# Three fp32r products in more places, context by columns, two load queues and another order in a fused attention and mixture-of-experts layer

## The chip, the cores and the metric
One core of one Trainium2 chip runs the kernel as one program. The metric is the device time of an execution in microseconds; lower is better. The engines are PE (TensorE, matmuls; its weight loads are listed as PEld), DVE (VectorE), ACT (ScalarE), POOL (GpSimd) and SP (SyncE, which here issues most DMAs). Each engine runs its own instructions in the order in which they are written, and semaphores tie the engines together.

## The reference
x is (32, 64, 128), that is 2048 tokens of width 128, in 32 sequences of 64. The context has the same shape. All is float32.

```python
# cross attention, 8 heads of width 128, q from layernorm(x), k and v from the context
q, k, v = xn @ Wq[h], ctx @ Wk[h], ctx @ Wv[h]            # per head h
A = softmax(mask(q @ k.T)); o = concat_h(A @ v); proj = o @ Wo
x1 = layernorm(ctx + proj) * gamma[0] + beta[0]
ffn = relu(x1 @ W1 + b1) @ W2 + b2                         # 128 -> 256 -> 128
x2 = x + layernorm(x1 + ffn) * gamma[1] + beta[1]
# mixture of experts on m = layernorm(x2)
scores = sigmoid(m @ router_w.T)                           # 16 experts in 4 groups
pick the best 2 groups, then the best 4 experts; combine = their scores, normalised, x 2.5
routed = sum_e combine[:, e] * ((silu(m @ gate_w[e]) * (m @ up_w[e])) @ down_w[e])
shared = silu(m @ sh_gate_w) * (m @ sh_up_w) @ sh_down_w   # two more "experts" of width 128
out = x2 + routed + shared
```

## The kernel before
**Tiling.** The 2048 tokens are 16 tiles of 128 (n = 0 to 15) and 4 chunks of 512 (c = 0 to 3). Everything stays in SBUF. Each engine's program is written out by hand as one list of calls of small helpers (`key`, `scores`, `attend`, `up`, `down`, ...), and each helper waits on counts of semaphores. So the order of work on an engine is the order of this list, and what an engine finds not ready holds up all behind it.

**Weights folded.** `fold` (PE) multiplies Wq with Wk and Wv with Wo per head. For the first product DVE's `centre` takes the mean off, ACT's `fold_high` rounds the result to fp32r (the high part) and DVE's `fold_low` subtracts to get the low part. `three` is a product in three fp32r passes, high x high, high x low and low x high, in place of one plain float32 matmul, which the profile lists as two instructions:

```python
pe.matmul(dst, w_hi, m_hi, start=start, stop=False)
pe.matmul(dst, w_hi, m_lo, start=False, stop=False)
return pe.matmul(dst, w_lo, m_hi, start=False, stop=stop)
```

**Attention.** Per chunk: POOL's `mask_context` multiplies the context rows by the mask, PE's `turn_ctx` transposes them (4 transposes), ACT's `cT_high` and DVE's `cT_low` split them, and `key(c, h)` makes the keys of head h with `three` (ACT copies each out of its bank, of which there are two). Per tile: `scores` (PE), `mask` and `maximum` (DVE), `subtract_max` (POOL), `exponent` (ACT), `sum_of_exp` (DVE), `normalise_probs` (POOL), `turn_probs` (PE transposes), `spread` (ACT copy), `attend` (PE, on context rows and on a copy with halves swapped), `heads_out` (ACT copies), `project` (PE), `add_ctx` (DVE). SRING = 3 score buffers are in use.

**Between attention and experts**, per chunk: `statistics(1)` (DVE), `inverse_root` (POOL), `normalise` (ACT), `turn_x1` (PE transposes into the post bank; ACT copies with a bias), `ffn_up(c, 0)` and `ffn_up(c, 1)` (PE, each followed by ACT's `hidden`), `ffn_down` (PE), `add_ffn`, `statistics(2)`, `residual`, `statistics(3)` (DVE), `normalise(3)`, `turn_xm` (PE transposes), `take_xm` (ACT copy), `route` (PE, router logits), `take_logits` (DVE), `mT_high` (ACT) and `mT_low` (DVE), the split of the transposed rows. Chunks 0 and 1 are routed together, then 2 and 3: `router_sigmoid` (ACT), `bias_scores`, `group_scores`, `keep_groups`, `keep_experts`, `combine` (DVE, some 45 small operations), `turn_combine` (PE), `take_combine` (DVE), a DMA to DRAM, and DMAs back that spread each expert's row over all partitions.

**Experts.** 18 experts (2 shared, 16 routed) x 4 chunks make N = 72 steps. Steps 0 to 35 do chunks 0 and 1, steps 36 to 71 chunks 2 and 3. The first four steps of a half are the shared experts: (0, c), (1, c), (0, c+1), (1, c+1); so step 2 is the first that needs chunk 1's rows. `up(n)` (PE) makes gate and up, each with `three` (6 passes); `gate` (ACT, silu), `gate_up` (DVE, product), for a routed expert `weigh` (POOL, times the combine weights), and `down(n)` (PE) into the chunk's bank. `up(n)` waits for the split `mT_low` of its chunk, and its second half for `gate_up(n - 2)`; `weigh(n)` waits for `down(n - 4)`. Down is a plain matmul up to step 35 and in the last three steps; in steps 36 to 68 it is `three`, for which ACT's `act_high` and DVE's `act_low` split its input and `dn_high` / `dn_low` the weights:

```python
return SPLIT_FROM <= n < SPLIT_TO     # 36 <= n < 69
```

**Loads.** ACT's queue issues context chunk 0, x by columns, and four quarters of w_in[0]. SP's queue waits for the second quarter and then issues x, context chunk 1, the mask, w_in[1] (two halves), the swapped context and the rest, last the staged expert weights w_gu and w_dn.

Of the kernel before, what the change touches and what calls it, by code (L numbers as in the profile page):

```python
# [57 lines left out]
def build(nc, x, x_cols, ctx_in, mask_tok, mask_pairs, w_attn, w_gu, w_dn, small, w1, w2, vec, out):  # L58
    es = ExitStack()
    with es:  # L60
# [23 lines left out]
        ctx_m = sb("ctx_m", [P, TPC, P])  # L84
# [190 lines left out]
        SPLIT_TO = N - 3  # L275

        def split(n):

            return SPLIT_FROM <= n < SPLIT_TO

        def split_count(n):

            return n - SPLIT_FROM + 1
# [35 lines left out]
        def _(sp):  # L319
# [1637 lines left out]
```

## Time and profile before
| | us |
|---|---|
| median of 3 runs | 296.77 (296.45 to 297.09) |
| the profiled execution, whole | 296.44 |
| its span, first to last instruction | 294.7 |
| PE busy | 285.2 (97%) |
| POOL busy | 183.4 (62%) |
| DVE busy | 178.1 (60%) |
| ACT busy | 161.0 (55%) |

The span is what the profile shows of an execution. The chain of waits follows the last instruction back to what released it, step by step; 88% of the span on it is PE. A timeline row gives the start, the duration, and in brackets how long the engine was idle ahead of it and what ended that. Durations of matmuls overlap (a pass of 0.39 us starts 0.23 us after the one ahead), so what a matmul costs PE is read from start to start. PE's granted clock is 1.00 (2.4 GHz) in every stretch.

### The profile page before, as it was taken

Reading aid. Unit: us, or ns where it says so; the run is one execution under the profiler, and the core shown is the slowest. Engines: PE = TensorE matmul, PEld = TensorE weight load, DVE = VectorE, ACT = ScalarE, POOL = GpSimd, SP = SyncE. Lnnn points to the kernel's source line nnn. Section 1 sums busy time; section 2 is a strip of 40 time slices with the busy share of each in tenths; the row PEclk is TensorE's granted clock in tenths of the full one; section 3 lists DMA queues with packets and bytes.
Section 4 is the critical chain, followed back from the end, with each engine's and each line's share of the span. In section 5 each row is a group of like instructions: output and inputs, shape, how many; then the busy total and the mean of one; then the engine's idle time right before and its main releaser. Section 6 shows DMA issues by size and latency. Waiting matters only on the chain.

```text
span 294.7 us, 4502 instructions
## 1 busy us (share of the span) xinstructions
PE 285.2 (97%) x1427; PEld 207.0 (70%) x1427; DVE 178.1 (60%) x476; ACT 161.0 (55%) x298; POOL 183.4 (62%) x167
## 2 busy tenths in 40 slices
PE   2999999999999999999999999999999999999995
PEld 2765667757776778867766766767668888888882
DVE  0757663837864775876654356397755766656561
ACT  2656667485578476955525352734274455555541
POOL 2136957446757487172758778766706788778871
PEclk9999999999999999999999999999999999999999
DMA  6899400000020000301762432320037236323202
GB/s 212 233 349 271 187 0 3 0 0 2 6 104 0 3 1 0 109 0 54 214 243 71 142 125 90 142 73 4 0 100 262 80 138 214 125 98 137 71 2 71
DMA packets 9575, 29.01 MB, mean 98 GB/s; under 512 B 1232, under 2 KB 2256, under 8 KB 9424
## 3 DMA queue, kind: packets, MB, share of 16 engines
q1 hardware_dynamic: 8688, 27.15, 27.5%
q10 hardware_dynamic: 864, 1.57, 1.6%
q8 instruction: 12, 0.20, 0.3%
q14 instruction: 11, 0.09, 0.1%
HBM read 27.54 MB, written 1.18 MB: 97 GB/s over the span
## 4 chain that ended last, share of the span: by engine, by line
PE 88%; DMA 4%; DVE 3%; ACT 1%; SPq 1%; issue 1%; ACTq 0%; DVEq 0%
PE bank L1449 16%; PE bank L1450 15%; PE bank L1451 15%; PE bank L1528 10%; PE bank L1655 10%; PE bank L1516 6%; PE bank L1488 6%; DMA w_in<-in_w_attn 4%; PE bank L1497 3%; PE bank L1557 3%; PE bank L1550 3%; PE bank L1579 1%; PE bank L1570 1%; PE bank L1543 1%; PE bank L1663 1%
## 5 line engine op out<-in xcount | busy, mean ns | idle before, releaser
L499 POOL TENSOR_TENSOR k_T<-x_T,k_T 128x512 f32<-128x512 f32 x64 | 94.2, 1480 | 41.8 <-DVE x_T L1229 23.1
L764 ACT ACTIVATE x_T<-bank 128x512 f32<-128x512 f32 x72 | 42.7, 598 | 69.5 <-PE bank L1451 68.4
L1229 DVE TENSOR_TENSOR x_T<-bank,x_T 128x512 f32<-128x512 f32 x64 | 43.7, 689 | 50.8 <-ACT x_T L764 27.6
L1449 PE MATMUL bank<-mT_hi,we_hi 128*128 128x512 f32 x144 | 62.7, 435 | 0.1
L1450 PE MATMUL bank<-mT_lo,we_hi 128*128 128x512 f32 x144 | 56.9, 395 | 0.0
L1451 PE MATMUL bank<-mT_hi,we_lo 128*128 128x512 f32 x144 | 56.9, 395 | 0.0
L1655 PE MATMUL bank<-k_T,w_in 128*128 128x512 f32 x78 | 36.6, 594 | 0.0
L1449 PEld LDWEIGHTS bank<-mT_hi,we_hi 128*128 128x128 f32 x144 | 27.1, 188 | 9.7 <-issue 3.8
L1528 PEld LDWEIGHTS bank<-vo,o_T 128*128 128x128 f32 x256 | 30.2, 192 | 4.2 <-issue 3.0
L1450 PEld LDWEIGHTS bank<-mT_lo,we_hi 128*128 128x128 f32 x144 | 27.1, 188 | 8.2 <-issue 2.9
L1528 PE MATMUL bank<-vo,o_T 128*128 128x128 f32 x256 | 31.9, 278 | 0.0
L1451 PEld LDWEIGHTS bank<-mT_hi,we_lo 128*128 128x128 f32 x144 | 27.0, 188 | 6.5
L666 ACT COPY k_T<-bank 128x512 f32<-128x512 f32 x32 | 18.7, 590 | 15.1 <-PE bank L1451 14.0
L421 POOL TENSOR_TENSOR sc_m<-sc_m,nmax 128x512 f32<-128x512 f32 x16 | 17.0, 1065 | 11.2 <-DVE nmax L1085 11.2
L1234 DVE TENSOR_TENSOR act_lo<-k_T,act_hi 128x512 fp32r<-128x512 f32 x33 | 22.5, 682 | 1.6 <-ACT act_hi L773 1.6
L429 POOL TENSOR_TENSOR prob<-sc_m,rsum 128x512 f32<-128x512 f32 x16 | 16.6, 1044 | 10.4 <-DVE rsum L1092 6.4
L695 ACT COPY o_T<-bank 128x512 f32<-128x512 f32 x32 | 17.9, 588 | 8.9 <-PE bank L1516 8.8
L1655 PEld LDWEIGHTS bank<-k_T,w_in 128*128 128x128 f32 x78 | 14.2, 190 | 11.4 <-issue 10.3
L405 POOL TENSOR_TENSOR rstd<-var_eps,neg_half 128x4 f32<-128x4 f32 x12 | 12.3, 1028 | 14.9 <-DVE var_eps L1048 14.9
L773 ACT CAST act_hi<-k_T 128x512 fp32r<-128x512 f32 x33 | 20.3, 614 | 0.3 <-DVE k_T L1229 0.3
L1078 DVE SCALAR_TENSOR_TENSOR sc_m<-bank,rstd_in,mask_add 128x512 f32<-128x512 f32 x16 | 12.0, 748 | 13.1 <-PE bank L1488 9.9
L1516 PE MATMUL bank<-prob_T,ctx_all 64*128 64x256 f32 x64 | 18.2, 402 | 0.0
(127 smaller groups left out, 486.1 us busy)
## 6 DMA issues: line engine op xcount, KB each, us to landing
k_T<-comb_dram SPq DMA_DIRECT2D x32, 512.0 KB, 3.7
w_in<-in_w_gu SPq DMA_DIRECT2D x3, 768.0 KB, 4.6
w_in<-in_w_dn SPq DMA_DIRECT2D x1, 1152.0 KB, 15.7
w_in<-in_w_attn ACTq DMA_DIRECT2D x4, 256.0 KB, 4.7
w_in<-in_w_attn SPq DMA_DIRECT2D x2, 512.0 KB, 7.6
ctx_swap<-in_ctx_in SPq DMA_DIRECT2D x2, 384.0 KB, 13.1
out_x<-ctx_all SPq DMA_DIRECT2D x3, 256.0 KB, 4.6
x_all<-in_x SPq DMA_DIRECT2D x2, 256.0 KB, 5.7
```

Source lines behind the costliest of these rows:

```text
L499: pool.tensor_tensor(act[n % 4], s_u[n % 2], comb[u % RING][:, c % 2 * CW:(c % 2 + 1) * CW], ALU.mult).then_inc(weighed_ready, 1)
L666: a.copy(k_T[c % 2][:, :, h, :], key_bank[i][:].rearrange("p (b s) -> p b s", s=SEQ)).then_inc(key_free[i], 1)
L764: a.activation(silu[n % 2], h_bank[n % 2][:], ACT.Silu).then_inc(silu_ready, 1)
L773: a.copy(act_hi[n % LAG][:], act[n % 4]).then_inc(act_hi_ready, 1)
L1229: v.tensor_tensor(into, u_bank[n % 2][:], silu[n % 2], ALU.mult).then_inc(s_u_ready, 1)
L1234: v.tensor_tensor(act_lo[n % LAG][:], act[n % 4], act_hi[n % LAG][:].bitcast(F32), ALU.subtract).then_inc(act_lo_ready, 1)
L1449: pe.matmul(dst, w_hi, m_hi, start=start, stop=False)
L1450: pe.matmul(dst, w_hi, m_lo, start=False, stop=False)
L1451: return pe.matmul(dst, w_lo, m_hi, start=False, stop=stop)
L1516: last = pe.matmul(o_bank[j][:].rearrange("p (h b s) -> p h b s", b=2, s=SEQ)[:, :, s, :], held[rows, n, :], prob_T[n % 2][rows, :, s, :], ...
L1528: last = pe.matmul(av_bank[:, 0:P], o_T[n % 2][:, h % 2, h // 2, :], vo[:, h, :], start=(h == 0), stop=(h == NH - 1))
L1655: pe.matmul(acc[c][:], dn[:, e, :], act[n % 4], start=start, stop=stop).then_inc(down_full, 1)
```

## The change
It makes five edits. (1) Steps 10 to 23 get the down product in three fp32r passes as well, with `act_high` and `act_low` for them. (2) The 8 `ffn_up` do the same: `w1_high` and `w1_low` split the weights once, and per chunk ACT writes `x1_hi` and a new DVE operation `x1_low` the rest. (3) Context chunks 1 to 3 are loaded by columns, already transposed, with the mask spread over the partitions by DMA; `turn_ctx` is left for chunk 0 alone, and `cT_high`/`cT_low` read SBUF. (4) Context chunk 0 goes first on SP's queue, and ACT's queue begins with the weights. (5) The lists of calls of all engines are in another order. Buffers are shared to make room (`ctx_m` with `xm_T`, `qk_c` with a `cen` buffer).

```diff
-        SPLIT_TO = N - 3
+        SPLIT = [*range(10, 24), *range(SPLIT_FROM, N - 3)]
...
         sp:
+            context(0, 1, ld_c0)
             sp.dma_start(mask_col[:], mask_tok).then_inc(ld_mask_col, 16)
+            def context_columns(c):
+                now = slice(c * CW, (c + 1) * CW)
+                if c > 1:
+                    sp.wait_ge(cT_ready, c - 1)
+                sp.dma_start(mask_r[:], mask_row[now].partition_broadcast(P)).then_inc(ld_cols[c], 16)
+                sp.dma_start(ctx_t[:], ctx_cols[:, now]).then_inc(ld_cols[c], 16)
             rows(0, 1, ld_x0)
-            context(1, 2, ld_c1)
+            context_columns(1)
...          (mask, w_in[1], swapped(0), rows(1), columns(1))
+            context(1, 2, ld_c1)
             context(2, CH, ld_c)
...          (the rest, small_T)
+            context_columns(2)
             sp.wait_ge(fold_done, 6)
...          (w_gu first batch, w_dn)
+                    context_columns(3)
...
         pool:
-            mask_context(0) mask_context(1) inverse_root(0, 0) mask_rows() mask_context(2)
+            mask_context(0) group_order() mask_context(1) mask_rows() inverse_root(0, 0)
...
+            normalise_probs(2) mask_context(2) normalise_probs(3) subtract_max(4)
...
         scalar:
-            a.dma_start(ctx_all[:, 0:TPC, :], ctx_in[:, 0:TPC, :]).then_inc(ld_c0, 16)
-            a.dma_start(x_T[:, 0:CW], x_cols[:, 0:CW]).then_inc(ld_xt[0], 16)
             for q in range(HP):
                 quarter(q)
+            a.dma_start(x_T[:, 0:CW], x_cols[:, 0:CW]).then_inc(ld_xt[0], 16)
...
-                a.activation(x1_T[:], post_bank[:], ACT.Identity, bias=bet[:, 0:1]).then_inc(post_free, 1)
+                a.activation(x1_hi[:], post_bank[:], ACT.Identity, bias=bet[:, 0:1]).then_inc(x1_hi_ready, 1)
+            def w1_high():
+                a.wait_ge(ld_ffn, 32)
+                a.copy(w1_hi[:], w1_in[:]).then_inc(w1_hi_ready, 1)
...
         vector:
+            def w1_low():
+                v.wait_ge(w1_hi_ready, 1)
+                v.tensor_tensor(w1_lo[:], w1_in[:], w1_hi[:].bitcast(F32), ALU.subtract).then_inc(w1_lo_ready, 1)
+            def x1_low(c):
+                v.wait_ge(x1_hi_ready, c + 1)
+                v.scalar_tensor_tensor(x1_lo[:], post_bank[:], bet[:, 0:1], x1_hi[:].bitcast(F32), ALU.add, ALU.subtract
+                                       ).then_inc(post_free, 1)
...
-            centre(0) cT_low(0) fold_low(0) centre(1) fold_low(1) centre(2) fold_low(2) centre(3) fold_low(3)
+            centre(0) fold_low(0) centre(1) cT_low(0) centre(2) fold_low(1) fold_low(2) centre(3) fold_low(3)
...          (hand-over to the experts)
+            statistics(3, 1) add_ctx(14) gate_up(0) add_ctx(15) statistics(1, 3) take_logits(1) gate_up(1)
+            mT_low(1) bias_scores(0) x1_low(2) group_scores(0) gate_up(2) keep_groups(0) keep_experts(0)
+            combine(0) take_combine(0) add_ffn(2) gate_up(3) statistics(2, 2) gate_up(4) x1_low(3) ...
...
         tensor:
-                pe.matmul(post_bank[:], w1_in[:, j * P:(j + 1) * P], x1_T[:],
-                          start=True, stop=True).then_inc(post_full, 1)
+                cols = slice(j * P, (j + 1) * P)
+                three(post_bank[:], w1_hi[:, cols], w1_lo[:, cols], x1_hi[:], x1_lo[:], True, True).then_inc(post_full, 1)
...          (start)
-            turn_ctx(0) fold(0, 0) fold(0, 1) fold(0, 2) fold(0, 3) key(0, 0) key(0, 1) ... key(0, 7)
-            fold(1, 0) turn_ctx(1) fold(1, 1) scores(0) key(1, 0) key(1, 1) scores(1) ...
+            fold(0, 0) fold(0, 1) turn_ctx() fold(0, 2) fold(0, 3) key(0, 1) key(0, 0) key(0, 2) ... key(0, 7)
+            fold(1, 0) scores(0) fold(1, 1) key(1, 0) scores(1) key(1, 1) key(1, 2) ...
...          (hand-over to the experts)
-            turn_probs(15) project(13) attend(14) turn_xm(1) up(1) route(1) project(14) attend(15) up(2)
-            turn_x1(2) up(3) project(15) down(0) down(1) ffn_up(2, 0) up(4) ffn_up(2, 1) down(2) ffn_down(2)
-            turn_combine(0) up(5) turn_x1(3) down(3) ffn_up(3, 0) up(6) ffn_up(3, 1) up(7) ffn_down(3) ...
+            attend(14) turn_probs(15) project(13) attend(15) project(14) up(1) project(15) turn_xm(1) route(1)
+            turn_x1(2) up(2) down(0) ffn_up(2, 0) down(1) up(3) up(4) down(2) ffn_up(2, 1) ffn_down(2)
+            turn_combine(0) up(5) turn_x1(3) down(3) up(6) ffn_up(3, 0) up(7) ffn_up(3, 1) up(8) down(4) ...
...          (steps 10 to 23)
+            up(14) up(15) down(10) up(16) down(11) down(12) up(17) up(18) route(2) down(13) up(19) down(14) up(20)
+            up(21) down(15) down(16) up(22) turn_xm(3) down(17) up(23) down(18) up(24) down(19) up(25) down(20)
+            route(3) down(21) up(26) up(27) up(28) down(22) down(23) ...
```
The lists of calls are written here several to a line; in the code each has its own.

## Rows read from the trace of the kernel before

**Rows 1.** The page, busy time by engine
```profile
PE 285.2 (97%) x1427; PEld 207.0 (70%) x1427; DVE 178.1 (60%) x476; ACT 161.0 (55%) x298; POOL 183.4 (62%) x167
```
**Rows 2.** Waits of PE: us in total, times, longest
```profile
PE bank L1461 <- POOL ctx_m L441: 5.7, 1, 5.7
```
**Rows 3.** Timeline of PE in steady steps of the second half: start, duration
```profile
258.93 0.39 PE L1449 MATMUL bank<-act_hi,key_room 128*128 128x512 f32 x1
...
259.61 0.40 PE L1449 MATMUL bank<-mT_hi,we_hi 128*128 128x512 f32 x1
```
**Rows 4.** The chain of waits: start, us, line, instructions
```profile
51.66 0.44 PE bank L1461 x4
...
66.17 0.86 PE bank L1550 x2
...
158.66 3.43 PE bank L1655 x8
```
**Rows 5.** Timeline of the start, PE and SP's queue
```profile
9.76 0.47 PE L1449 MATMUL bank<-key_room 128*128 128x512 f32 x1
10.07 0.39 PE L1450 MATMUL bank<-cT_lo,key_room 128*128 128x512 f32 x1
...
17.23 0.60 PE L1461 MATMUL bank<-ident,ctx_m 128*128 128x128 f32 x4
...
17.89 1.16 PE L1595 MATMUL bank<-w_in 128*128 128x128 f32 x8
...
19.08 0.33 SPq L359 DMA_DIRECT2D w_in<-in_w_gu  x1
```
**Rows 6.** Busy time by stretch, columns PE, PEld, DVE, ACT, POOL, clock, DMA, GB/s
```profile
20.00:30.00 10.00, 10.00 (x45) 5.62 (x44) 8.33 (x21) 6.05 (x12) 6.09 (x6) 1.00 1.05 310
...
157.00:192.00 35.00, 35.00 (x138) 23.65 (x137) 17.17 (x41) 18.19 (x36) 27.09 (x26) 1.00 0.33 120
```
**Rows 7.** DMA issues of the first 20 us: KB, us to landing
```profile
w_in<-in_w_gu SPq DMA_DIRECT2D x1, 768.0 KB, 13.3
```
**Rows 8.** Groups of POOL in 157 to 192 and in 230 to 280 us
```profile
L499 POOL TENSOR_TENSOR k_T<-x_T,k_T 128x512 f32<-128x512 f32 x15 | 19.4, 1310 | 7.6 <-PE bank L1655 5.6 <-DVE x_T L1229 1.9
...
L499 POOL TENSOR_TENSOR k_T<-x_T,k_T 128x512 f32<-128x512 f32 x25 | 41.9, 1676 | 10.5 <-DVE x_T L1229 10.5
```
**Rows 9.** Timeline of the hand-over, all engines
```profile
116.11 0.66 PE L1570 MATMUL bank<-ident,cen 128*128 128x128 f32 x4
...
116.80 0.59 ACT L727 COPY xm_T<-bank 128x512 f32<-128x512 f32 x1
...
117.99 0.96 PE L1579 MATMUL bank<-small_T,xm_T 128*128 128x16 f32 x8
118.08 1.36 DVE L1106 TENSOR_TENSOR mT_lo<-xm_T,mT_hi 128x512 fp32r<-128x512 f32 x1 [2.63 <-ACT mT_hi L731]
...
122.64 0.26 DVE L1158 TENSOR_TENSOR k_T<-k_T 128x96 f32<-128x96 f32 x1
...
130.92 1.02 PE L1550 MATMUL bank<-x_T,w_in 128*128 128x512 f32 x2
...
132.72 2.05 PE L1557 MATMUL bank<-w_in,hid 128*128 128x128 f32 x16
...
134.61 0.27 PE L1607 MATMUL bank<-ident,comb_w 128*128 128x128 f32 x1
...
135.41 0.28 DVE L1216 COPY comb_T<-bank 128x128 f32<-128x128 f32 x1
...
141.51 1.28 POOL L499 TENSOR_TENSOR k_T<-x_T,k_T 128x512 f32<-128x512 f32 x1 [0.71 <-DMA k_T<-comb_dram]
```
**Rows 10.** Timeline of the second routing, PE and DVE
```profile
189.05 0.96 PE L1579 MATMUL bank<-small_T,xm_T 128*128 128x16 f32 x8
...
190.10 0.21 DVE L1111 COPY logits<-bank 128x64 f32<-128x64 f32 x1
...
192.56 1.24 DVE L1158 TENSOR_TENSOR k_T<-k_T 128x96 f32<-128x96 f32 x1
```

More of the change, by code:

```diff
@@ L55, with build @@
 VEC = 4 + P + NE
-def build(nc, x, x_cols, ctx_in, mask_tok, mask_pairs, w_attn, w_gu, w_dn, small, w1, w2, vec, out):
+def build(nc, x, x_cols, ctx_in, ctx_cols, mask_row, mask_tok, mask_pairs, w_attn, w_gu, w_dn, small, w1, w2, vec, out):
     es = ExitStack()
@@ L802, in _ @@
             cT_high(1)
+            key(1, 0)
             fold_high(4)
-            key(1, 0)
-            fold_high(5)
+            exponent(0)
             key(1, 1)
@@ L1004, in _ @@
             gate(41)
-            for n in range(42, N):
+            act_high(40)
+            gate(42)
+            act_high(41)
+            gate(43)
+            act_high(42)
+            gate(44)
+            act_high(43)
+            gate(45)
+            act_high(44)
+            gate(46)
+            act_high(45)
+            gate(47)
+            act_high(46)
+            gate(48)
+            act_high(47)
+            gate(49)
+            act_high(48)
+            gate(50)
+            act_high(49)
+            gate(51)
+            act_high(50)
+            gate(52)
+            act_high(51)
+            gate(53)
+            act_high(52)
+            gate(54)
+            act_high(53)
+            gate(55)
+            act_high(54)
+            gate(56)
+            act_high(55)
+            gate(57)
+            act_high(56)
+            gate(58)
+            act_high(57)
+            gate(59)
+            act_high(58)
+            gate(60)
+            act_high(59)
+            gate(61)
+            act_high(60)
+            gate(62)
+            act_high(61)
+            gate(63)
+            act_high(62)
+            gate(64)
+            act_high(63)
+            gate(65)
+            act_high(64)
+            gate(66)
+            act_high(65)
+            gate(67)
+            act_high(66)
+            gate(68)
+            act_high(67)
+            gate(69)
+            act_high(68)
+            gate(70)
+            for n in range(71, N):
                 gate(n)
@@ L1415, in _ @@
             gate_up(33)
+            mT_low(3)
+            take_combine(1)
             gate_up(34)
-            mT_low(3)
             gate_up(35)
@@ L1430, in _ @@
             gate_up(41)
-            for n in range(42, N):
+            act_low(40)
+            gate_up(42)
+            add_out(1)
+            act_low(41)
+            gate_up(43)
+            act_low(42)
+            gate_up(44)
+            act_low(43)
+            gate_up(45)
+            for n in range(46, N):
                 gate_up(n)
@@ L1739, in _ @@
             turn_x1(0)
-            key(3, 0)
+            project(4)
+            scores(10)
+            ffn_up(0, 0)
+            key(3, 2)
             key(3, 1)
-            ffn_up(0, 0)
-            scores(10)
-            turn_probs(7)
             ffn_up(0, 1)
```

639 lines of the change are left out of this document (339 added, 300 removed).

## The prediction
> **What bounds the kernel now.** I read the page first, then the waits of PE, then the chain of waits, then timelines at the places that the diff touches. PE is busy for 285.2 us of the 294.7 us span [rows 1]. It sits idle 5.7 us before its first instruction [rows 2] and for a few us in the drain at the end, and hardly anywhere else. The chain of waits that ended last runs through PE for 88% of the span. So PE is the bound, and two questions decide: how much PE time goes, and whether the new order leaves PE something to do at each wait. "Busy" can't be used for the first, since the durations of matmuls overlap. I use the distance from start to start, or the pieces of the chain, which don't overlap.
>
> **PE time that goes.** A down in three products: from its first pass to the next up is 0.68 us [rows 3]. Four plain downs (8 instructions) take 3.43 us, so one takes 0.857 [rows 4]. 14 downs (steps 10 to 23) x 0.175 = 2.45 us. A plain `ffn_up` takes 0.86 [rows 4]; three passes at 0.23 take 0.69, and where the work ahead of them is of another kind the first pass takes 0.31 for 0.23 [rows 3, 5]. 8 x 0.17 less 0.1 at some of them: 1.2 us (0.6 to 1.4). `turn_ctx` of chunks 1 to 3: the first takes 17.23 to 17.89, 0.66 us with a wait of 0.2 for the second half of the weights in it [rows 5], two more take 0.44 [rows 4]: 1.5 us.
>
> **The start.** The context now goes on SP's queue while ACT's queue begins with the weights, so `fold(0, 0)` need not follow `turn_ctx` (5.68 us [rows 2]). But the first key needs `cT_low(0)`, which DVE now runs after `fold_low(0)` and `centre(1)`: by my walk at 9.5 us against 9.76 [rows 5]. After that ACT waits for `key(0, 0)`, which PE now runs second, and holds `fold_high(2)` behind it. I count 0.5 us of gain (0 to 1.2), small gaps between the first keys included. On SP, `context_columns(1)` adds one DMA and 256 KB ahead of `mask_add` and of the second weights. Those landed just in time at 17.89 [rows 5]; `fold(1, 1)` now comes after `scores(0)` (1.01 us) and is covered by as much. Later SP issues `context_columns(2)` before w_gu and w_dn: 0.75 MB more ahead of w_dn, at the 310 GB/s that moved in 20 to 30 us 2.4 us [rows 6]. w_gu landed 13.3 us after its issue at 19.08, at 32.4 [rows 5, 7]; its first reader, `split_hi(0)`, stands where PE is at about 36 us. `mask_context(2)` waits on POOL for the columns, and behind it stand `normalise_probs(3)` and `subtract_max(4)`. By the same bytes they land by 34 us; PE wants `turn_probs(3)` at about 38. So I cost the loads at nothing; without that cover each late us is one us.
> The Trainium skill ("DMA: Bandwidth & Descriptors", Issuing engines are not separate DMA queues) says that DMAs of different engines run on the same 16 DMA engines and only issue time is saved. By that rule the second queue gives one issue, 0.4 us, and the start not more; no row here has the two queues starting together, and the sum above does without it.
>
> Sum of what goes: 2.45 + 1.2 + 1.5 + 0.5 = 5.65 us (4.5 to 6.6).
>
> **What is added off PE.** 14 `act_high` on ACT (0.6 us), 14 `act_low` on DVE (0.68), 4 `x1_low` and one `w1_low` on DVE, `w1_high` on ACT. In 157 to 192 us, which is now up to 2.5 us shorter, ACT is busy 18.2 of 35 us and DVE 17.2, so both have room for 8 to 10 us [rows 6]. POOL is busy 27.1 there. Its `weigh` takes 1310 ns there, and 1676 ns in 230 to 280 us, where `act_low` runs beside it [rows 8]. 14 x 0.37 = 5.1 us more, less `dn_low(2)`, `add_b2(3)` and one `inverse_root`, which move ahead (4 us): 28 of 32.5 us. Downs stay 4 to 5 ups behind, over 7 us, and weigh, cast and subtraction take under 4. I take 0.3 us for it.
>
> **What the order exposes.** Here I expect most of the gain to go. Before, the tail of attention (`project(14)`, `attend(15)`, `project(15)`, `up(1)`) was spread between the steps of chunk 1's hand-over to the experts, and each wait had cover. After, PE runs all of it first, then `turn_xm(1)`, `route(1)`, `turn_x1(2)`, `up(2)`, `down(0)`, ... From the start T of `turn_xm(1)`:
> - `route(1)` follows at once. It needs `take_xm(1)`: ACT starts it 0.69 us after the transposes start and takes 0.59 [rows 9]. Route at T+1.33, PE free at 0.44: 0.89 us idle. Before, `up(1)` lay between.
> - `turn_x1(2)` waits for `take_logits(1)`: DVE starts that 1.05 us after a route starts, 0.21 long (189.05, 190.10) [rows 10]. T+2.64, PE free at 2.14: 0.50.
> - `up(2)` (step 2 is chunk 1's first) waits for `mT_low(1)`, on DVE behind `gate_up(1)`: 0.60 + 0.69 after the logits. T+3.95, PE free at 3.08: 0.87. Before, it ran in 118.08 to 119.44, and `project(14)` and `attend(15)` stood ahead of `up(2)` [rows 9].
> - `ffn_down(2)` now directly follows `ffn_up(2, 1)`. Before, the up began at 130.92 and took 0.86, ACT made `hidden` of it, and `ffn_down` began at 132.72, 0.94 us after the up's end, with `down(2)` in between [rows 9]. Now 0.94 is exposed.
> - `turn_combine(0)`: from `route(1)`'s start to it PE has about 13.7 us with these waits, where it had 16.6 (117.99 to 134.61) [rows 9]. DVE's routing: `bias_scores` 1.5 us from T+4.1, `x1_low` 0.65, `group_scores` 0.9, `gate_up(2)` at 7.6 (behind ACT's `split_hi(6)`, `dn_high(2)` and a table load), `keep_groups` 2.2, `keep_experts` 2.2, `combine` 1.5 to 2.2: T+14.2 to 14.9, and PE's `ffn_down(2)` ends at T+15. Just hidden; 0 to 1.1.
> - `up(5)`: its second half needs `gate_up(3)`, which DVE now runs after `take_combine(0)` and `add_ffn(2)`. 0.3 + 0.2 + 0.6 + 0.69 = 1.8 us after the transpose starts, PE has 0.8 us of work: 1.0. Before, DVE ran `gate_up(3)` ahead of both.
> Sum: 0.89 + 0.50 + 0.87 + 0.94 + 1.0 = 4.2 us, and 0.3 for routing operations that meet POOL. The waits of combine weights (before: 135.41 to `weigh(4)` at 141.51, 6.1 us [rows 9]) stay covered: `up(8)` is the first to need them. Elsewhere each pair of dependent steps has cover.
>
> Time: the profiled execution's own 296.44 (span 294.7 and 1.7 around it) - 5.65 + 4.5 + 0.3 = 295.6. The median of the runs, 296.77, is 0.33 above the profiled one: 295.9.
>
> **Rivals.**
> A, the forecast: 295.2 to 296.6. 0.45.
> B, the hand-over costs little: the waits shown above are filled, for instance because PE arrives at T late by something else and DVE and ACT are ahead; under 2.5 us lost, 292 to 294.5. For it: before, DVE and ACT were idle in half of this stretch. Against it: four of the five waits start from PE's own result, and so don't shrink. 0.16.
> C, the full gain, 291.3: all waits hidden. It needs PE's list to be other than the diff shows. 0.06.
> D, DVE and POOL block each other, and the new time is not below the old. After the hand-over POOL has `split_lo(6)`, `add_b2(2)` and `dn_low(2)` back to back just where DVE does `group_scores`; before, POOL was nearly idle there. An operation of 96 columns took 0.26 us at 122.64 and 1.24 us at 192.56, when POOL was at work [rows 9, 10]. Two or three such hits add 1 to 3 us ahead of `turn_combine(0)`, and in steps 10 to 23 the longer `weigh` adds 0 to 2. From 0.9 us in all the change gains nothing; 296.7 to 299, middle 297.3. 0.28.
> The Trainium skill ("SBUF — State Buffer", SBUF: two separate sides) says that DVE with two SBUF inputs and POOL share a port pair by an exclusive lock. That is D's mechanism, the trace agrees at 192.56, and by it alone the time would be D's.
> E, an early load is late (POOL at `mask_context(2)`, or ACT at `split_hi(0)`): over 300. It decides from 38 us on; bytes say 34. 0.05.
>
> **How the numbers follow.** Likeliest A, 295.9. The range 292.6 to 298.2 takes in most of B, A, and D up to its middle and 1 us beyond; it leaves out C, E and D's end, under 2 in 10. A alone: 295.2 to 296.6. 0.2% is 0.6 us, about what this measurement can tell from no change: faster is below 296.2. A gives 0.30 faster, 0.15 same; B and C 0.22 faster; D 0.10 same, 0.18 slower; E 0.05 slower: 0.52, 0.25, 0.23.
>
> **What would show it.** Right: PE idle before `route(1)`, `turn_x1(2)`, `up(2)`, `ffn_down(2)` and inside `up(5)`, 0.5 to 1 us each, 4 to 5 us in all, within 18 us; downs 10 to 23 at 0.68 us; PE's distance from first to last instruction shorter by about 1 us. Wrong: no such gaps (B, C), a gap above 1 us before `turn_combine(0)` or between steps 10 and 23 (D), or PE idle before 60 us (E). If `fold(1, 0)` starts well before 16.2 us, the start is mis-sized.

## The result: 0.8% slower, and the profile after

The changed kernel takes 299.37 us (median of 6 runs, 298.52 to 299.96) against 296.81 for the kernel before on the same chip: the ratio is 1.008, with a 95% interval of 1.0066 to 1.0094. The forecast was 295.9 us with a range up to 298.2, so the time is outside it, on the far side. The profiled execution took 299.96 us, the longest of the six, and its span is 298.0. One execution of e1 (978.8 us) and one of e6 (468.41 us, mean granted clock 0.56), two of the kernels below, are left out of all medians and ratios.

The page of the changed kernel, busy time by engine:
```profile
PE 282.1 (95%) x1437; PEld 210.2 (71%) x1437; DVE 200.8 (67%) x495; ACT 172.0 (58%) x313; POOL 189.3 (64%) x167
...
PE 85%; DVE 8%; ACT 3%; issue 2%; DMA 1%; DVEq 0%; POOL 0%; POOLq 0%
```
Against [rows 1] PE is busy 3.1 us less while the span is 3.3 us longer, and DVE is 22.7 us busier. The second line is the chain of waits by engine: 85% PE where it was 88, and 8% DVE. So work did leave PE, and more than that came back as waiting. The waits of PE (us in total, times, longest), where the kernel before had the first instruction's 5.7 us [rows 2], 0.5 us in the drain and nothing else above 0.1:
```profile
PE bank L1728 <- DMA w_in<-in_w_attn: 5.1, 1, 5.1
PE bank L1581 <- DVE x_T L1333: 1.1, 2, 0.9
PE bank L1581 <- DVE x_lo L1195: 1.0, 1, 1.0
PE bank L1581 <- DVE key_room L1222: 1.0, 2, 0.6
PE bank L1581 <- DVE k_T L1333: 0.9, 1, 0.9
PE bank L1690 <- ACT hid L735: 0.8, 1, 0.8
PE bank L1581 <- ACT k_T L677: 0.8, 1, 0.8
PE bank L1712 <- ACT xm_T L743: 0.7, 1, 0.7
...
PE bank L1676 <- DVE logits L1215: 0.4, 1, 0.4
```
They lie in three places. To size each I use three marks that stand in the same place of the work in all kernels, each read from one profiled execution: the start of `fold(1, 0)`, of `up(13)` and of `up(35)`. From `up(35)` on the two traces run in step to the end.

| start of | before | after | difference in the stretch | forecast for it |
|---|---|---|---|---|
| `fold(1, 0)` | 16.35 | 18.16 | +1.81 | -0.5 |
| `up(13)` | 153.90 | 157.58 | +1.87 | +1.8 (4.2 + 0.3 - 1.5 - 1.2) |
| `up(35)` | 209.58 | 212.77 | -0.49 | -2.15 (0.3 - 2.45) |

The middle line came out as forecast, though by two errors that cancel; the first and the last did not.

**The start.** Timeline of the first keys in the changed kernel, all engines:
```profile
9.69 0.76 PE L1581 MATMUL bank<-key_room 128*128 128x512 f32 x1
...
11.65 1.07 ACT L677 COPY k_T<-bank 128x512 f32<-128x512 f32 x2 [2.27 <-PE bank L1583]
...
12.38 0.47 PE L1581 MATMUL bank<-key_room 128*128 128x512 f32 x1 [0.77 <-ACT k_T L677]
...
12.61 0.42 ACT L753 CAST key_room<-cen 128x256 fp32r<-128x256 f32 x1
12.81 1.30 POOL L447 TENSOR_TENSOR ctx_t<-ctx_t,mask_r 128x512 f32<-128x512 f32 x1 [5.98 <-DMA ctx_t<-in_ctx_cols]
...
13.06 1.33 DVE L1222 TENSOR_TENSOR key_room<-cen,key_room 128x256 fp32r<-128x256 f32 x1 [2.40 <-ACT key_room L753]
...
14.44 0.50 PE L1581 MATMUL bank<-key_room 128*128 128x512 f32 x1 [0.45 <-DVE key_room L1222]
...
18.16 1.05 PE L1728 MATMUL bank<-w_in 128*128 128x128 f32 x8
```
The first key starts at 9.69, close to the 9.5 of my walk and to [rows 5]. From it to `fold(1, 0)` it took 6.59 us before and takes 8.47 now: the chain slips. PE makes `key(0, 1)` first and `key(0, 0)` second, but ACT's list takes `key(0, 0)` first, so both copies begin after the second key, at 11.65. Behind them stand the next key's free bank (0.77 us of PE) and `fold_high(2)` at 12.61. That makes `fold_low(2)` start at 13.06, just after POOL's multiplication of the context columns (12.81 to 14.11), and it takes 1.33 us where the first takes 0.43; `fold_low(3)`, at 15.65, takes 0.95. PE waits 0.45 and 0.56 us for the two.

**The hand-over**, from the start T = 121.40 of `turn_xm(1)`:
```profile
122.68 1.06 PE L1712 MATMUL bank<-small_T,xm_T 128*128 128x16 f32 x8 [0.67 <-ACT xm_T L743]
...
124.15 0.63 PE L1676 MATMUL bank<-ident,cen 128*128 128x128 f32 x4 [0.41 <-DVE logits L1215]
...
125.30 0.48 PE L1581 MATMUL bank<-mT_hi,we_hi 128*128 128x512 f32 x1 [0.53 <-issue]
...
126.56 1.27 POOL L489 TENSOR_TENSOR we_lo<-w_in,we_hi 128x512 fp32r<-128x512 f32 x1 [0.84 <-ACT we_hi L774]
...
126.72 1.26 DVE L1256 TENSOR_TENSOR k_T<-k_T,vec_row 128x128 f32<-128x128 f32 x1
...
128.01 0.75 DVE L1195 SCALAR_TENSOR_TENSOR x_lo<-bank,vec_row,x_hi 128x512 fp32r<-128x512 f32 x1
...
128.82 0.50 PE L1581 MATMUL bank<-x_hi,w_hi 128*128 128x512 f32 x1 [1.02 <-DVE x_lo L1195]
...
135.76 2.05 PE L1690 MATMUL bank<-w_in,hid 128*128 128x128 f32 x16 [0.78 <-ACT hid L735]
...
139.50 0.50 PE L1581 MATMUL bank<-mT_hi,we_hi 128*128 128x512 f32 x1 [0.88 <-DVE k_T L1333]
```
The five waits of the forecast are all there: `route(1)`, `turn_x1(2)`, `up(2)`, `ffn_down(2)` and the second half of `up(5)`. The brackets count from the modelled end of the matmul ahead, the forecast from where PE could have started the next one; counted like the forecast they are 0.84, 0.66, 0.71, 0.95 and 1.05 us, 4.2 in all for the forecast's 4.2. The sixth, 1.02 us (1.18 counted like the forecast) of `ffn_up(2, 0)` for `x1_low(2)`, I had costed at nothing: a routing operation of 128 columns took 1.26 us beside POOL's `we_lo`, and `x1_low(2)` came behind it. The stretch from T to the end of `up(5)` lasts 18.9 us, and 5.4 of it are these six waits.

### The profile page after: what moved, and what is told of

It is laid out like the page before. It is cut to its first block, busy times and chain, and to the rows that moved or that the text cites. A ratio compares the mean times of both kernels' runs of the same rounds, so it can differ in the third digit from the quotient of the medians.

```text
span 298.0 us, 4604 instructions
## 1 busy us (share of the span) xinstructions
PE 282.1 (95%) x1437; PEld 210.2 (71%) x1437; DVE 200.8 (67%) x495; ACT 172.0 (58%) x313; POOL 189.3 (64%) x167
## 3 DMA queue, kind: packets, MB, share of 16 engines
q10 hardware_dynamic: 720, 1.31, 1.2%
HBM read 29.12 MB, written 1.18 MB: 102 GB/s over the span
## 4 chain that ended last, share of the span: by engine, by line
PE 85%; DVE 8%; ACT 3%; issue 2%; DMA 1%; DVEq 0%; POOL 0%; POOLq 0%
PE bank L1581 17%; PE bank L1582 16%; PE bank L1583 16%; PE bank L1661 10%; PE bank L1788 6%; PE bank L1649 6%; PE bank L1619 5%; PE bank L1628 3%; PE bank L1690 3%; DVE act_lo L1338 2%; PE bank L1728 2%; DMA w_in<-in_w_attn 1%; DVE x_T L1333 1%; PE bank L1703 1%; PE bank L1796 1%
## 5 line engine op out<-in xcount | busy, mean ns | idle before, releaser
L509 POOL TENSOR_TENSOR k_T<-x_T,k_T 128x512 f32<-128x512 f32 x64 | 97.1, 1525 | 39.1 <-DVE x_T L1333 27.2
L1581 PE MATMUL bank<-mT_hi,we_hi 128*128 128x512 f32 x144 | 60.0, 417 | 2.5 <-DVE x_T L1333 1.1
L1338 DVE TENSOR_TENSOR act_lo<-k_T,act_hi 128x512 fp32r<-128x512 f32 x47 | 42.1, 906 | 2.1 <-ACT act_hi L792 2.1
L792 ACT CAST act_hi<-k_T 128x512 fp32r<-128x512 f32 x47 | 28.9, 619 | 15.2 <-POOL k_T L509 14.5
L416 POOL TENSOR_TENSOR rstd<-var_eps,neg_half 128x4 f32<-128x4 f32 x12 | 13.3, 1104 | 24.6 <-DVE var_eps L1140 24.5
L1788 PE MATMUL bank<-k_T,w_in 128*128 128x512 f32 x50 | 23.4, 592 | 0.0
L1581 PE MATMUL bank<-act_hi,key_room 128*128 128x512 f32 x47 | 18.7, 398 | 0.0
L1583 PE MATMUL bank<-act_hi,dn_lo 128*128 128x512 f32 x47 | 18.4, 391 | 0.0
```

The source lines that it names most:

```text
L509: pool.tensor_tensor(act[n % 4], s_u[n % 2], comb[u % RING][:, c % 2 * CW:(c % 2 + 1) * CW], ALU.mult).then_inc(weighed_ready, 1)
L792: a.copy(act_hi[n % LAG][:], act[n % 4]).then_inc(act_hi_ready, 1)
L1338: v.tensor_tensor(act_lo[n % LAG][:], act[n % 4], act_hi[n % LAG][:].bitcast(F32), ALU.subtract).then_inc(act_lo_ready, 1)
L1788: pe.matmul(acc[c][:], dn[:, e, :], act[n % 4], start=start, stop=stop).then_inc(down_full, 1)
```

## The experiments

Each is timed against the kernel before, in five rounds. The last three columns are starts in one profiled execution of each (before: 16.35, 153.90, 209.58), and the text calls the last of them the trace. The start of the kernel varies from one execution to the next: `fold(1, 0)` is at 18.16, 17.63, 17.72 and 16.78 in the changed kernel, e2, e3 and e5, which run the same lists up to there. So a difference in that column alone is no effect of an edit; the distances between marks, and the waits at a place, are the better evidence.

| run | us, median | ratio to before (95%) | `fold(1, 0)` | `up(13)` | `up(35)` |
|---|---|---|---|---|---|
| changed kernel | 299.37 | 1.008 (1.0066 to 1.0094) | 18.16 | 157.58 | 212.77 |
| e1 keys in order | 298.42 | 1.0053 (1.0035 to 1.0071) | 16.14 | 155.78 | 210.93 |
| e2 hand-over covered | 298.25 | 1.0048 (1.0028 to 1.0068) | 17.63 | 156.09 | 211.19 |
| e3 plain downs 10 to 23 | 300.5 | 1.0121 (1.009 to 1.0152) | 17.72 | 157.53 | 214.15 |
| e4 edits in the old order | 314.41 | 1.0581 (1.0544 to 1.0619) | 18.80 | 166.81 | 226.90 |
| e5 POOL moved | 297.86 | 1.0028 (1.0006 to 1.005) | 16.78 | 156.55 | 210.67 |
| e6 = e1 + e2 + e5 | 294.71 | 0.9931 (0.9908 to 0.9953) | 16.42 | 152.45 | 207.16 |
| e7 = e6, plain downs | 295.56 | 0.996 (0.9943 to 0.9976) | 16.29 | 152.24 | 207.88 |
| e8 POOL held at the start | 298.85 | 1.0067 (1.0041 to 1.0093) | 17.43 | 156.86 | 211.99 |
| e9 = e6 + gate_up(26) earlier | 294.7 | 0.9917 (0.9894 to 0.9939) | 17.50 | 153.95 | 208.07 |
| e10 = e6, plain ffn_up | 294.96 | 0.9932 (0.9913 to 0.9951) | 16.98 | 153.83 | 208.53 |
| e11 = e6, old queues | 296.23 | 0.998 (0.9962 to 0.9998) | 19.16 | 155.22 | 209.94 |
| e12 = e9 + e8 | 293.58 | 0.9893 (0.9869 to 0.9916) | 16.07 | 152.20 | 206.33 |

### e1: the keys in order
```diff
-            key(0, 1)
             key(0, 0)
+            key(0, 1)
```


> The changed kernel (299.4 us) with one exchange: PE makes key(0, 0) before key(0, 1), as the kernel before did. Theory S (the order of these two keys costs the start): ACT takes key(0, 0) first and both fold_high(2) and the next keys stand behind it. With the exchange the first copy starts about 0.97 us after the first key (10.7 instead of 11.65), fold_high(2) at 11.9, fold_low(2) ends at 12.8 just before POOL's multiplication of the context columns starts, the pairs of keys follow at 1.7 us, and fold(1, 0) starts at 16.3 instead of 18.16: 297.6 us. Rival P (the meeting of DVE and POOL costs it): fold_low(2) and fold_low(3) still take 1.3 and 0.95 us for 0.43, and only the first 0.9 us comes back: 298.5 us. Rival L (a load or the context columns set the end of the start anyway): 299.4 us.

Timeline of e1:
```profile
10.51 1.28 ACT L677 COPY k_T<-bank 128x512 f32<-128x512 f32 x2 [1.40 <-PE bank L1583]
...
12.13 0.43 DVE L1222 TENSOR_TENSOR key_room<-cen,key_room 128x256 fp32r<-128x256 f32 x1 [1.73 <-ACT key_room L753]
...
12.72 1.28 POOL L447 TENSOR_TENSOR ctx_t<-ctx_t,mask_r 128x512 f32<-128x512 f32 x1 [6.01 <-DMA ctx_t<-in_ctx_cols]
```
`fold_low(2)` now ends 0.16 us before POOL starts, and `fold(1, 0)` is at 16.14, 6.71 us behind the first key (9.43) and not 8.47: theory S, in this profile. `up(35)` comes 1.84 us sooner in the trace, but the median fell by 0.9 only, to 298.42, and that is rival P's number. Part of the difference is which executions were profiled (the changed kernel's is 0.6 us above its median, e1's 0.4 below). Another part may be the small margin of 0.16 us, though no run of e1 shows it: in the profiles of e9 and e10, which have the keys in order too, `fold_low` met POOL again and PE waited 0.56 and 0.33 us for it.

### e8: POOL held back at the start, keys as changed
```diff
+            pool.wait_ge(fold_lo, 4)
             mask_context(1)
```


> The changed kernel, keys in its own order, with POOL's mask_context(1) and all behind it held until fold_low(3) is done. It splits the loss of the start in two: the order of the keys (copies 0.95 us later) stays, the meeting of fold_low(2) and fold_low(3) with POOL (1.33 and 0.95 us for 0.43) goes. If both count, fold(1, 0) starts 0.8 to 1.0 us earlier than 18.16: 298.5 us. If POOL's part is hidden, 299.4; if holding POOL delays the context columns or the first mask, scores(1) or key(1, 0) waits, and the time is 299.4 or more.

298.85 us, between the forecasts of 298.5 and 299.4; `fold(1, 0)` starts at 17.43, 0.73 us sooner behind a first key at the same 9.69, and the two waits for `fold_low` are gone while the 0.77 us for the copy stays. So the two causes of the start are the order of the keys and, through it, the meeting with POOL. How they share the loss varies: in e5's profile `fold_low` happened not to meet POOL, and from the first key to `fold(1, 0)` it took 7.25 us (7.74 in e8). The order alone costs 0.7 to 1.2 us over the 6.59 before, the meeting 0.7 to 1.2.

### e2: the hand-over with cover
```diff
 PE   attend(15) project(14) up(1)
-     project(15) turn_xm(1) route(1) turn_x1(2) up(2) down(0) ffn_up(2, 0) down(1) up(3) up(4) down(2)
-     ffn_up(2, 1) ffn_down(2) turn_combine(0)
+     turn_xm(1) project(15) route(1) down(0) turn_x1(2) up(2) down(1) ffn_up(2, 0) up(3) up(4) ffn_up(2, 1)
+     down(2) ffn_down(2) turn_combine(0)
 DVE  statistics(3, 1) ahead of add_ctx(13); gate_up(1), mT_low(1), add_ctx(15), take_logits(1),
      statistics(1, 3) in this order; gate_up(3) ahead of take_combine(0)
 ACT  gate(1) ahead of take_xm(1)
```


> The changed kernel with the hand-over to the experts given its cover again: PE runs up(1) and project(15) around turn_xm(1) and down(0) after route(1), up(3) and up(4) ahead of ffn_up(2, 1), down(2) between ffn_up(2, 1) and ffn_down(2); DVE runs statistics(3, 1) before add_ctx(13), mT_low(1) before the logits, gate_up(3) before take_combine(0). Theory H (each wait is a pair of dependent steps without cover): PE's idle time between turn_xm(1) and the end of up(5) falls from 5.5 us to about 1.5: 295.4 us. Rival R (the routing chain on DVE, slowed by POOL, sets the end of the stretch): PE's waits move to turn_combine(0) or to up(8), and less than 1.5 us comes back: 298 us or more.

This is nearer the rival. The five waits are gone and 0.38 us for `x1_low(2)` is left, but two new ones of 1.5 and 1.4 us stand in their place (timeline of e2, POOL, DVE and PE):
```profile
125.88 1.27 POOL L489 TENSOR_TENSOR we_lo<-w_in,we_hi 128x512 fp32r<-128x512 f32 x1
...
126.17 1.10 DVE L1262 TENSOR_TENSOR k_T<-k_T 128x96 f32<-128x96 f32 x1
...
127.12 1.30 POOL L463 TENSOR_TENSOR x_b<-cen,b_beta 128x512 f32<-128x512 f32 x1
...
127.19 1.33 DVE L1263 TENSOR_TENSOR k_T<-k_T 128x64 f32<-128x64 f32 x1
...
128.38 1.28 POOL L499 TENSOR_TENSOR dn_lo<-w_in,key_room 128x512 fp32r<-128x512 f32 x1
...
128.42 1.31 DVE L1264 TENSOR_TENSOR k_T<-k_T 128x32 f32<-128x32 f32 x1
...
130.91 0.49 PE L1581 MATMUL bank<-mT_hi,we_hi 128*128 128x512 f32 x1 [1.53 <-DVE k_T L1333]
...
136.75 0.33 PE L1740 MATMUL bank<-ident,comb_w 128*128 128x128 f32 x1 [1.36 <-DVE comb_w L1313]
```
Three operations of 96, 64 and 32 columns take as long as POOL's three of 512, one beside each. In [rows 9] the one of 96 columns took 0.26 us.

### e5: POOL's operations moved out of the routing
```diff
-            split_lo(6); add_b2(2); dn_low(2)       (behind inverse_root(1, 3))
+            pool.wait_ge(route_step, 11)            (keep_groups(0) done)
+            add_b2(2); split_lo(6)
+            pool.wait_ge(route_done, 1)
+            dn_low(2)
...
             weigh(25)
+            split_lo(8)
```


> The changed kernel (299.4 us) with three things moved on POOL's list alone: add_b2(2) and split_lo(6) wait until keep_groups(0) is done, dn_low(2) until combine(0) is done, and split_lo(8) runs after weigh(25) and not after weigh(28). Theory M (DVE's small two-input operations take 1.2 to 1.4 us when POOL works beside them and 0.3 us alone): the routing operations of the first routing take 0.3 us, x1_low(2) is done 1.0 us sooner and ffn_up(2, 0) no longer waits; in the second routing the last three operations of keep_groups fall to 0.3 us and PE's 0.85 and 0.23 us at 194 and 204 us go: 297.3 us. Rival N (the long operations come from something else, or hide behind PE's work anyway): 299.2 to 299.5 us.

DVE in the same place:
```profile
126.31 0.25 DVE L1264 TENSOR_TENSOR k_T<-k_T 128x96 f32<-128x96 f32 x1
126.47 0.24 DVE L1265 TENSOR_TENSOR k_T<-k_T 128x64 f32<-128x64 f32 x1
126.61 0.21 DVE L1266 TENSOR_TENSOR k_T<-k_T 128x32 f32<-128x32 f32 x1
```
Theory M for the mechanism: 0.25, 0.24 and 0.21 us. The combine weights are ready 3.1 us sooner (134.4 for 137.5; 1.4 of it from the start), `ffn_up(2, 0)` doesn't wait, and from `up(13)` to `up(35)` the trace is 1.07 us shorter. (The keys happened not to meet POOL in this profile, so the start gave 1.4 us by itself.) But from `fold(1, 0)` to `up(13)` it got 0.35 us longer. The windows of e5 (us, then busy time of PE, PEld, DVE, ACT, POOL, then PE's granted clock) show why:
```profile
122.00:124.00 2.00, 1.06 (x9) 0.79 (x8) 1.84 (x5) 1.97 (x4) 1.73 (x3) 1.00 0.05 14
124.00:126.00 2.00, 2.00 (x6) 1.56 (x7) 1.80 (x5) 1.98 (x5) 0.26 (x2) 0.56 0.00 0
126.00:128.00 2.00, 2.00 (x5) 1.10 (x4) 1.54 (x6) 1.53 (x2) 0.00 (x0) 0.59 0.00 0
128.00:130.00 2.00, 2.00 (x9) 1.30 (x8) 1.86 (x8) 0.00 (x0) 0.00 (x0) 1.00 0.00 0
```
After the 2 us in which PE was busy for 1.06, its clock fell from 1.00 to about half, 1.2 GHz, for some 3 us: the passes of `up(2)` start 0.43 us apart and not 0.23. `up(2)` takes 2.46 us where it took 1.48, and `down(0)` with the first pass behind it 1.71 where 1.09 is usual (129.62 to 130.71 in the changed kernel). That is some 1.5 us, and it ate the 1.2 that the edit had freed at `ffn_up(2, 0)`.

### e6: all three


> The changed kernel with all three amendments: the two keys in order, the hand-over with its cover, and the moves on POOL's list. The hand-over's edit alone gave only 1.1 us in the trace, since three routing operations of 1.1 to 1.3 us each beside POOL made up(4) and turn_combine(0) wait 1.5 and 1.4 us. Theory M: with POOL quiet there, these waits go as well: 298.25 (hand-over edited alone) less 1.3 (what is left of the start), less about 3.0 (waits of the hand-over), less 1.2 (second routing): 292.7 us, 4 us below the kernel before. Rival R (the chain from the logits to the combine weights is too long in itself): PE still waits for 1.5 us or more before turn_combine(0) or for weigh(4): 294.5 us or more.

294.71 us, 0.7% below the kernel before. e2 alone shortened the stretch from `fold(1, 0)` to `up(13)` by 0.96 us and e5 alone lengthened it by 0.35; together (136.03 us against 139.42) they shorten it by 3.4, and the clock is 1.00 throughout. By its time this is the rival's (294.5 or more), by what PE waits for it is theory M, 2 us short: `turn_combine(0)` waits 0.63 us for the combine weights and not 1.5, 0.38 us for `x1_low(2)` stay, and so does the changed kernel's 0.85 us inside `up(28)`, which had gone in e5's profile.

### e3 and e7: the splits of steps 10 to 23 undone
```diff
-        SPLIT = [*range(10, 24), *range(SPLIT_FROM, N - 3)]
+        SPLIT = [*range(SPLIT_FROM, N - 3)]
```
(and the 14 `act_high` and 14 `act_low` of these steps taken out), in the changed kernel (e3) and in e6 (e7).

> The changed kernel with plain downs in steps 10 to 23 (no act_high, no act_low there), all else kept. Theory G (the 14 casts and subtractions crowd DVE, ACT and POOL and give back 1.9 of the 2.45 us): PE gets 2.45 us more work and loses the 1.9 us of gaps at 180, 187, 193 and 204 us: 299.9 us. Rival F (these gaps belong to the order, with or without the splits): 301.8 us.

> The kernel with all three amendments, but with plain downs in steps 10 to 23. If the casts and subtractions no longer cost anything once POOL is out of the way, the splits are worth their full 14 x 0.175 = 2.45 us here: 295.1 us. If they cost in steps 10 to 23 what they cost in the changed kernel (where they were worth 1.4 us in the trace), 294.1 us.

e3 costs 1.4 us in the trace from `up(13)` to `up(35)` (56.62 for 55.19), between the two theories. Of the 1.2 us of waits at 180 to 205 us, 1.08 are there without the splits as well, so most of these belong to the order; and the splits were worth 1.4 and not 2.45. Counted from start to start the 14 split downs take 9.97 us (0.68 to 0.79 each), and the plain ones of e3, with what they add to the pass behind them, 12.0: that is 2.0 us. The waits counted the same way are 1.9 us with the splits and 1.25 without: the other 0.6. e7 fell on neither side: with POOL out of the way the splits were worth 0.7 us in the trace and 0.85 by the medians (294.71 against 295.56), less than before. The reason is the wait inside `up(28)`, which e6 has and e7 does not. Timeline of e6, POOL, DVE and PE:
```profile
184.51 2.99 POOL L509 TENSOR_TENSOR k_T<-x_T,k_T 128x512 f32<-128x512 f32 x2
...
184.52 3.52 DVE L1340 TENSOR_TENSOR act_lo<-k_T,act_hi 128x512 fp32r<-128x512 f32 x2
...
188.11 0.67 DVE L1335 TENSOR_TENSOR x_T<-bank,x_T 128x512 f32<-128x512 f32 x1
...
188.83 0.50 PE L1583 MATMUL bank<-mT_hi,we_hi 128*128 128x512 f32 x1 [0.85 <-DVE x_T L1335]
```
`act_low(22)` and `(23)` take 1.76 us each beside `weigh`, where they take 0.68 alone, and `gate_up(26)`, which PE waits for, stands behind them.

### e9: gate_up(26) ahead of act_low(23)


> The kernel with all three amendments (294.8 us), and on DVE gate_up(26) ahead of act_low(23) and take_logits(3). There PE waited 0.85 us inside up(28) for gate_up(26), which stood behind two act_low of 1.76 us each and the logits, while POOL was at work. Theory C (that wait is the price of the splits' crowding, and nothing else is late behind it): the 0.85 us goes, 294.0 us, and the splits are then worth 1.6 us against plain downs (295.6). Rival D (the second routing only starts later and the wait comes back at up(29) or up(33)): 294.8 us.

The wait of 0.85 us goes and 0.28 comes back at `up(32)`: from `up(13)` to `up(35)` 54.12 us for 54.71, between C and D. The medians (294.7 and 294.71) don't tell the two apart; in its profile the start was late (`fold(1, 0)` at 17.50). Against e7 (55.64) the splits are now worth 1.5 us in the trace.

### e10: ffn_up plain again
```diff
-                three(post_bank[:], w1_hi[:, cols], w1_lo[:, cols], x1_hi[:], x1_lo[:], True, True)
+                pe.matmul(post_bank[:], w1_in[:, cols], x1_hi[:], start=True, stop=True)
```
(with `x1_hi` in full float32, and without `w1_high`, `w1_low` and `x1_low`)

> The kernel with all three amendments (294.8 us), but ffn_up as a plain matmul again (no w1_high, w1_low, x1_low). By the start-to-start distances PE gets 8 x 0.15 = 1.2 us more work; the wait of 0.38 us for x1_low(2) goes: 295.7 us. If the other x1_low crowd DVE elsewhere (as the 14 act_low do), less: 295.0 us or below.

From `fold(1, 0)` to `up(13)` 136.85 us for 136.03: the three products are worth 0.8 us in the trace, as expected: 1.2 of PE's work less the 0.38 us that chunk 2's first `ffn_up` waits for `x1_low(2)`. By the medians the difference (0.25 us) is within the noise, on the side of "less".

### e11: the old queues
```diff
-            context(0, 1, ld_c0)                                  (SP)
+            a.dma_start(ctx_all[:, 0:TPC, :], ...)                (ACT, ahead of the weights)
+            a.dma_start(x_T[:, 0:CW], ...)
```
(and turn_ctx, cT_high(0) and cT_low(0) in their old places)

> The kernel with all three amendments (294.8 us), but with the context of chunk 0 and x on ACT's queue ahead of the weights, and turn_ctx first on PE, cT_high(0) first on ACT and cT_low(0) second on DVE, as in the kernel before: edit 4 undone. The first key then starts at 9.75 us again where the traces with the keys in order had it at 9.43 to 9.7: 0.1 to 0.3 us later, 295.0 us. If the second queue brought what I counted (0.5 us), 295.3; if it brought nothing, 294.8.

Worse than each forecast: 296.23 us, 1.5 more than e6. PE waits for both parts of the weights:
```profile
7.49 0.79 PE L1730 MATMUL bank<-w_in 128*128 128x128 f32 x2 [0.74 <-DMA w_in<-in_w_attn]
...
19.16 1.16 PE L1730 MATMUL bank<-w_in 128*128 128x128 f32 x8 [1.64 <-DMA w_in<-in_w_attn]
```
The second wait, 1.64 us for w_in[1], is the cost. SP's list goes on when the second quarter of the first weights has landed: at 8.11 us here and at 5.47 in e6, and it issues w_in[1], behind the 512 KB of `context_columns(1)`, that much later (10.72 for 8.01). But the order of the queues does not explain all of it. ACT issues the first weights at the same times as in the kernel before (1.70 us on), behind the same two DMAs, and they land later. The four quarters, issue to landing, in the kernel before and in e11:
```profile
DMA to landing us min/median/max: 4.1/4.7/4.9
...
DMA to landing us min/median/max: 5.7/6.0/6.2
```
SP went on at 6.80 us in the kernel before. So of e11's 2.6 us against e6, 1.3 are loads that moved more slowly, for a reason that no run shows; e4, the other run with the old queues and the columns, has 5.7/6.0/6.2 too. The profiled execution is also one of e11's longest (297.2; they range from 294.99 to 297.29). The Trainium skill ("DMA: Bandwidth & Descriptors", Issuing engines are not separate DMA queues) allows a second queue only its issue time. Between the kernel before and the changed one the traces nearly agree: the weights are issued 0.9 us sooner, and SP goes on 1.1 us sooner (5.70 for 6.80; 1.3 in e6).

### e4: the edits in the old order
Edits 1 to 3 in the lists and queues of the kernel before; `mask_context(2)` moved behind `normalise_probs(0)`, `dn_low(2)` behind `dn_low(1)`, `up(6)` and `up(7)` ahead of the `ffn_up` of chunk 3, `act_high(n)` and `act_low(n)` behind `gate(n + 2)` and `gate_up(n + 2)`.

> The edits in the products and the context by columns (edits 1 to 3) put into the order and the two load queues of the kernel before; only what needs it is moved (mask_context(2), dn_low(2), up(6) and up(7) ahead of the two ffn_up of chunk 3). Theory O (the new order ate the gain): PE's work falls by 2.45 + 1.2 + 1.5 = 5.15 us and next to nothing new waits: 291.7 to 292.3 us. Rival G (the 14 casts and subtractions crowd the engines in any order): 1.9 us less gain, 293.6 us. Rival X (the gain of each edit is smaller than the start-to-start distances say, or PE waits elsewhere as before): 295 us or more.

314.41 us: theories O and G fell, and X (295 or more, PE waits elsewhere) is right in kind and 19 us short. Waits of PE in e4:
```profile
PE bank L1514 <- DVE act_lo L1280: 3.9, 4, 1.6
PE bank L1552 <- DVE sc_m L1113: 2.9, 1, 2.9
PE bank L1514 <- DVE x_lo L1137: 2.8, 2, 2.3
PE bank L1661 <- DMA w_in<-in_w_attn: 2.0, 3, 0.8
```
The 2.9 us is POOL's `mask_context(2)`, which stood ahead of a `normalise_probs` and waited until 34.23 us for columns issued at 21.23: rival E's mechanism, in another list. Each split down that followed an up too closely cost 0.7 to 1.6 us. Besides, PE's clock fell twice, behind the waits of 2.9 and 2.3 us (last section). So the edits can't be priced in the old order, and they need a new one; what e1, e2 and e5 mend are a few places in it.

### e12: e9 with POOL held at the start


> The kernel with the three amendments and gate_up(26) moved (294.7 us), and POOL's mask_context(1) held until fold_low(3) is done. In its profile fold_low(3) still met POOL at the start and PE waited 0.56 us for it; in the profile of the version before it did not, so the meeting falls in some executions and not in others. Theory M (holding POOL takes the meeting away in every execution): no wait for fold_low, the spread of the runs narrows, 294.2 us. Rival L (the wait for the second half of the first weights, 0.2 to 0.5 us in these profiles, takes its place, since PE comes to fold(1, 0) sooner): 294.6 us. Rival H (the context columns are now masked too late for cT_high(1), at about 15.7 us, or the first mask waits): key(1, 0) or scores(1) waits, 294.7 us or more.

293.58 us (4 executions), 1.1% below the kernel before, and 1.9% below the changed kernel by the two ratios. No `fold_low` meets POOL, no wait for w_in[1] above 0.12 us is left, and what remains of PE's waits is 0.64 (combine weights), 0.40 (`cT_low(0)`), 0.38 (`x1_low(2)`), 0.29 and 0.19 us. Theory M, with 0.6 us more than it expected; the 0.6 is not explained.

## Why the prediction was wrong

Three terms failed: the start (forecast 0.5 us of gain, 1.8 lost), `x1_low(2)` in the hand-over (nothing, 1.2 us), and the stretch with steps 10 to 23 (forecast 2.45 of gain less 0.3, got 0.5). DVE's operations beside POOL's have a part in all three. Against them stand 0.8 us of gain that I had not counted.

**The PE time that goes** was sized rightly for one instruction and wrongly for the whole of the splits. A down of steps 10 to 23 takes 0.68 us and an `ffn_up` 0.80 (63.85 to 64.65) where it follows other work. But 4 of the 14 downs take 0.76 to 0.79 in the changed kernel, and all 14 together save 2.0 us of PE's work, not 2.45. With their waits the splits brought 1.4 us there and 1.5 at best (e9 against e7).

**The start is the step that failed first.** "I count 0.5 us of gain (0 to 1.2)": it lost 1.81. The walk to the first key was right, and I saw that ACT waits for `key(0, 0)`, "which PE now runs second", with `fold_high(2)` behind it. I gave that no price. It costs about 0.95 us at the copies, and by delaying `fold_high(2)` it moves `fold_low(2)` under POOL's multiplication, another 0.7 (e8). In e1's profile the exchange of two lines takes both back; the median moved by about half of that.

**The hand-over** was right in kind and in its five sizes (0.84, 0.66, 0.71, 0.95, 1.05 found; 0.89, 0.50, 0.87, 0.94, 1.0 forecast, and `route(1)` starts at T + 1.28 for 1.33). `x1_low(2)` at nothing was wrong: 1.18 us, from POOL. Sum 5.4 for 4.5. That `up(13)` came out right is luck: from `fold(1, 0)` to there 0.8 us more of the gain arrived than I counted. Sorted by kind of matmul, from start to start, it lies in attention, at the transposes of the probabilities (8.15 us before, 7.72 after) and at `project` (29.62 and 29.12); what freed it is not shown.

**Steps 10 to 23 at 0.3 us** was the second step that failed. Counted from start to start PE waits 1.9 us there; 1.25 of it is there without the splits (e3), at the second routing, which meets POOL, and 0.6 comes with them. I took `act_low` at 0.68 us from a stretch where it has room; here, beside `weigh`, the 14 took 1.35 us on average (18.5 us in all). I had looked at POOL's busy time and at how much `weigh` would lengthen, and not at what POOL does to DVE. In 160 to 175 us DVE is busy 14.0 us of 15, where it was 5.5. What is late then is a `gate_up`, and PE with it.

**Rival D** was nearest, and the time is above its range too (296.7 to 299), which the order of the keys, that it did not have, can account for. Its mechanism is in all three places, and e2, e5 and e6 show it directly. The Trainium skill ("SBUF — State Buffer", SBUF: two separate sides) describes it as an exclusive lock for a whole instruction, and the trace agrees: a DVE operation of 32 columns, 0.21 us alone, takes 1.31 beside one of POOL, while `x1_low`, which reads one of its inputs from PSUM, takes 0.75 either way. Its place and size I had half wrong: at the start I had not looked for it at all. **E** did not happen here (no wait at 30 to 45 us), and happened in e4. **B** and **C** are out for this list; e12 reaches 293.6, in B's range, by filling the waits that B had thought filled.

## What to carry to other kernels

Where every engine runs a written list, compare the order of each pair of lists that pass buffers to each other: one key made before its neighbour, taken after it, cost a whole copy and moved what followed under another engine's work. Price every small two-input DVE operation at the length of the POOL operation that may stand beside it, above all in a chain; then ask which list can be moved so that they don't meet. And price an edit's cover where it will run: work that is "free" on an engine at half load was 1.35 us and not 0.7 each at full load.

## What I had not expected of the hardware

PE's granted clock fell to about half (0.50 to 0.59, the 1.2 GHz level) for some 3 us in three of the profiles (e1, e3, e5), each time in the hand-over, at or behind the waits of 0.4 to 0.7 us ahead of `route(1)`, `turn_x1(2)` and `up(2)` (in e1 behind the first two), and not in e2, e6 or e12, where these waits are filled. In e4 it fell twice elsewhere, behind single waits of 2.93 us (to 38.34) and 2.33 us (to 105.26), and all six of its executions have a mean clock of 0.982 to 0.988. Windows of e4, columns as above:
```profile
40.00:42.00 2.00, 2.00 (x9) 1.71 (x8) 1.90 (x10) 1.22 (x2) 2.00 (x2) 0.51 0.37 123
...
108.00:110.00 2.00, 2.00 (x7) 1.39 (x6) 1.81 (x4) 0.00 (x0) 1.05 (x1) 0.50 0.00 0
```
In e5 the executions with a mean clock of 0.997 or more took 296.35 to 297.81 us (5 runs) and those with 0.992 or 0.993 took 297.8 to 299.25 (7 runs). So a cluster of short waits can cost more than their sum. In e1 it cost nothing that the times show (8 executions at 0.991 to 0.994: 298.03 to 299.31 us; 3 at 0.999 or more: 298.06 to 299.10): in its profile the slow passes fill the time that `ffn_up(2, 0)` would else wait for `x1_low(2)`. And it does not happen in every execution: the changed kernel's own profile has the same waits and a clock of 1.00.

And two edits that each brought little or nothing between `fold(1, 0)` and `up(13)` (-1.0 us, and +0.35 with the fallen clock in it) brought 3.4 us together.
